# Moving the subtraction of the maximum from ScalarE to GpSimd in 48 of 128 attention units

## The reference, cut to what matters

```
# block 0                                       # block 1
scores = q @ k.T + mask                         scores = clip(q @ k.T * scale, -100, 100); masked: -inf
weights = softmax(scores, axis=-1)              attn = softmax(scores, axis=-1)
out = relu((weights @ v) @ wo.T + wo_b)         out = (attn @ v) @ wo.T + bo
```

## Time and profile before

| | us |
|---|---|
| median of 3 runs | 2119.77 |
| lowest, highest | 2115.42, 2124.47 |
| the profiled execution | 2117.64 |
| its span, first to last instruction | 2115.9 |
| busy in the span: PE, DVE, ACT, POOL | 1859.6, 1486.2, 1302.6, 616.5 |

### The profile page before, as it was taken

One profiled execution on the slowest core, in us unless ns is written; L12 is line 12 of the kernel. 1 busy time (PEld: TensorE's weight loads), 2 busy tenths in 40 slices (PEclk: granted clock), 3 DMA queues, 4 the chain that ended last, 5 costly groups with the idle time before them and its releaser, 6 DMA issues.

```text
span 2115.9 us, 49981 instructions
## 1 busy us (share of the span) xinstructions
PE 1859.6 (88%) x17665; PEld 1511.9 (71%) x17669; DVE 1486.2 (70%) x3873; ACT 1302.6 (62%) x4466; POOL 616.5 (29%) x610
## 2 busy tenths in 40 slices
PE   3998999989999897577898889999999998898879
PEld 2777888878888775455666677787777777677665
DVE  5898887878888785757666675767757565654556
ACT  1987766656667786456577766667666654544432
POOL 0003031322322220034333343254452523233321
PEclk9999999999999999868699999999999999999999
DMA  8013455444644001300000011222222223232351
GB/s 245 17 31 105 126 163 156 134 136 140 181 133 127 26 26 50 110 20 20 30 7 15 7 46 50 83 75 89 79 74 69 76 87 91 71 103 70 110 155 43
DMA packets 128789, 178.44 MB, mean 84 GB/s; under 512 B 10144, under 2 KB 89824, under 8 KB 128288
## 3 DMA queue, kind: packets, MB, share of 16 engines
q1 hardware_dynamic: 120864, 159.51, 25.0%
q0 software_dynamic: 7680, 15.74, 2.4%
HBM read 141.26 MB, written 33.95 MB: 83 GB/s over the span
## 4 chain that ended last, share of the span: by engine, by line
PE 38%; DVE 9%; ACT 6%; issue 4%; POOL 1%; DMA 0%; DVEq 0%; ACTq 0%; SPq 0%
PE ps L1674 5%; PE ps L1959 5%; PE ps L1907 3%; PE ps L1712 3%; PE ps L1900 3%; ACT pb L2108 3%; PE ps L1696 3%; PE ps L1881 2%; PE ps L1703 2%; PE ps L1685 2%; PE ps L1722 1%; DVE nm L2487 1%; PE ps L1730 1%; PE ps L1929 1%; PE ps L1873 1%
## 5 line engine op out<-in xcount | busy, mean ns | idle before, releaser
L2108 ACT ACTIVATE pb<-ps,nm 128x128 f32<-128x128 f32 x1024 | 363.1, 377 | 192.6 <-DVE nm L2487 192.5
L2156 POOL TENSOR_TENSOR pb<-pb,rcs 128x512 f32<-128x512 f32 x256 | 268.3, 1049 | 667.1 <-DVE rcs L2495 666.2
L986 ACT ACTIVATE pb<-pb,nm 128x128 f32<-128x128 f32 x1024 | 312.9, 393 | 30.9 <-DVE nm L1221 29.1
L2512 DVE COPY pt<-ps 128x512 f32<-128x512 f32 x128 | 88.3, 690 | 203.6 <-PE ps L1959 203.4
L2108 ACT ACTIVATION_READ_ACCUMULATOR pb<-ps,nm 128x1 f32 x1024 | 221.3, 216 | 0.0
L2487 DVE TENSOR_REDUCE nm<-ps 128x8 f32<-128x1024 f32 x128 | 155.9, 1218 | 62.2 <-PE ps L1907 39.0
L1959 PE MATMUL ps<-w,pb 128*128 128x128 f32 x1024 | 168.7, 290 | 21.9 <-ACT pt L2116 10.8
L1221 DVE TENSOR_REDUCE nm<-pb 128x8 f32<-128x1024 f32 x128 | 156.2, 1220 | 4.4
L1959 PEld LDWEIGHTS ps<-w,pb 128*128 128x128 f32 x1024 | 122.4, 148 | 46.3 <-ACT pt L2116 20.3
L870 PE MATMUL ps<-w,pb 128*128 128x128 f32 x1024 | 141.8, 280 | 8.2 <-ACT pb L986 7.9
L2116 ACT ACTIVATE pt<-ps 128x512 f32<-128x512 f32 x128 | 76.9, 601 | 94.9 <-PE ps L1959 94.6
(11 more groups left out here) (379 smaller groups left out, 4405.0 us busy)
## 6 DMA issues: line engine op xcount, KB each, us to landing
big<-in_we SPq DMA_DIRECT2D x92, 514.0 KB
big<-in_we SPq DMA_DIRECT2D x109, 384.0 KB
sorted_out<-big SPq DMA_DIRECT2D x27, 256.0 KB
big<-sorted_in SPq DMA_DIRECT2D x7, 960.0 KB, 5.7
sorted_in<-big SPq DMA_DIRECT2D x4, 1472.0 KB, 12.1
big<-sorted_in SPq DMA_DIRECT2D x20, 256.0 KB, 3.8
hidden<-h_all SPq DMA_DIRECT2D x7, 512.0 KB, 3.0
h_all<-hidden SPq DMA_DIRECT2D x7, 512.0 KB, 3.7
```

The costliest lines, as they stand in the source:

```text
L986: m = a.activation(pb[:, n % 2, k * S:(k + 1) * S], pb[:, n % 2, k * S:(k + 1) * S], ACT.Exp, bias=nm[:, n % 2, k:k + 1])
L2108: m = a.activation(pb[:, n % 2, e * S:(e + 1) * S], ps[:, score_bank(n) + half, k * S:(k + 1) * S], ACT.Exp, bias=nm[:, n % 2, e:e + 1], a ...
L2156: g_.tensor_tensor(p4, p4, r4.unsqueeze(2).to_broadcast([P, 4, S]), ALU.mult).then_inc(n2["p_normed"], 1)
L2512: v.tensor_copy(pt[:, p % 2, 4 * S:8 * S], ps[:, BANK_T, :]).then_inc(n2["p_lo"], 1)
```

## The change

In the units 1 to 26 and 106 to 127 (`SHIFTED`) the eight exponentials on ACT go. In their place POOL adds the negated maxima to the masked scores, in place in `pb`, in two instructions of 128 x 512 (four heads each). PE turns these shifted scores instead of the exponentials, and ACT forms the exponential while it empties the PSUM banks into `pt`, with the instructions that were copies before. The other 80 units (`BIASED`) stay as they were. Waits on the exponentials become waits on either semaphore (`formed`). To make room in POOL's order, the power for the front layernorm moves from unit 1 of a stream to unit 0 (from the third group on), ahead of the subtraction; and the eight gathers of the last group, which were four in unit 7 of stream 13 and four in unit 0 of stream 14 (steps 111 and 112), become two in each of the steps 110 to 113, behind the subtraction of their step.

```diff
+        GATHERS = [{-1: range(G), 0: range(G, 2 * G)}] * (NG - 1) + [{at: range(2 * at + 4, 2 * at + 6) for at in range(-2, 2)}]
+        SHIFTED = [n for n in range(NUN) if 1 <= n <= 26 or n >= 106]
+        BIASED = [n for n in range(NUN) if n not in SHIFTED]
...
+        def formed(n, half=1):
+            of = SHIFTED if n in SHIFTED else BIASED
+            return s["shifted" if n in SHIFTED else "exps"], 2 * of.index(n) + 1 + half
...
-                                pe.wait_ge(s["exps"], 2 * p + 1 + k // 4)
+                                pe.wait_ge(*formed(p, k // 4))
...
-                        a.activation(pt[:, p % 2, 0:4 * S], ps[:, 2, :], ACT.Copy).then_inc(s["p_hi"], 1)
+                        to_pt = ACT.Exp if p in SHIFTED else ACT.Copy
+                        a.activation(pt[:, p % 2, 0:4 * S], ps[:, 2, :], to_pt).then_inc(s["p_hi"], 1)
...
-                            a.activation(pt[:, p % 2, 4 * S:8 * S], ps[:, 3, :], ACT.Copy).then_inc(s["p_lo"], 1)
+                            a.activation(pt[:, p % 2, 4 * S:8 * S], ps[:, 3, :], to_pt).then_inc(s["p_lo"], 1)
                     work(1, n)
-                    if n < NUN:
+                    if n in BIASED:
                         a.wait_ge(s["maxed"], n + 1)
...
+                def shift(n):
+                    g_.wait_ge(s["maxed"], n + 1)
+                    for half in range(2):
+                        p4 = pb[:, n % 2, 4 * half * S:4 * (half + 1) * S].rearrange("p (k s) -> p k s", k=4)
+                        m4 = nm[:, n % 2, 4 * half:4 * half + 4]
+                        g_.tensor_tensor(p4, p4, m4.unsqueeze(2).to_broadcast([P, 4, S]), ALU.add)\
+                            .then_inc(s["shifted"], 1)
...
-                    if layer == 1 and u == 0:
-                        gather(g, range(G, 2 * G))
-                    if layer == 0 and u == 1:
+                    if layer == 0 and u == (0 if g > 1 else 1):
                         pow_(front, g + 1)
+                    if n in SHIFTED:
+                        shift(n)
+                    if layer == 1 and u in GATHERS[g]:
+                        gather(g, GATHERS[g][u])
...
-                    if layer == 1 and u == 7:
-                        g_.wait_ge(moe["stored"], 16 * NQ0 * (g // 2 + 1))
...
-                        gather(g, range(G))
+                    if layer == 1 and u - NU in GATHERS[g]:
+                        if min(GATHERS[g]) == u - NU:
+                            g_.wait_ge(moe["stored"], 16 * NQ0 * (g // 2 + 1))
...
+                        gather(g, GATHERS[g][u - NU])
...
-                            v.wait_ge(s["exps"], 2 * (n - 1))
+                            v.wait_ge(*formed(n - 2))
```

More of the change, by code:

```diff
@@ L297, in build @@
                       "p_lo", "pv", "o_recip", "normed", "oT_psum", "oT_ready", "out_psum", "bias_added"]
-        att_a = attention_sems("a", both_kinds + ["q_ready", "masked", "o_read", "o_turned"])
+        att_a = attention_sems("a", both_kinds + ["q_ready", "masked", "shifted", "o_read", "o_turned"])
         att_b = dict(att_a, **attention_sems("b", ["sums_turned", "p_normed", "k3_psum", "k3_col", "v_row", "chunk_added",
@@ L628, in build @@
                     last_evacuated = (moe["hid_dve" if k % 2 else "hid_act"], k // 2 + 1)
+        s = att_a
         spare_slots = h_all[:, 0:12, :].rearrange("p (a b) t -> p a b t", b=3)
@@ L1041, in _ @@
                     layer, g = stream(j + 2)
-                    if layer == 1 and u == 7:
-                        g_.wait_ge(moe["stored"], 16 * NQ0 * (g // 2 + 1))
-                        if g:
-                            g_.wait_ge(moe["gathered"], 16 * 2 * G * g)
-                            g_.wait_ge(moe["combined"], g)
-                        gather(g, range(G))
+                    if layer == 1 and u - NU in GATHERS[g]:
+                        if min(GATHERS[g]) == u - NU:
+                            g_.wait_ge(moe["stored"], 16 * NQ0 * (g // 2 + 1))
+                            if g:
+                                g_.wait_ge(moe["gathered"], 16 * 2 * G * g)
+                                g_.wait_ge(moe["combined"], g)
+                        gather(g, GATHERS[g][u - NU])
                 g_.wait_ge(moe["gathered"], 16 * 2 * G * NG)
```

## The result

Beside the kernel before on the same chip the changed kernel took 2136.5 us (median of 7 runs) against 2115.42: ratio 1.0105, interval 1.0086 to 1.0124. It is slower by 1.0%, as forecast (2140, range 2116 to 2160). The profiled execution took 2131.53 us, its span is 2129.8.

What follows compares the result with a forecast made beforehand. Plain units were taken to be at PE's floor of 3.77 us, loaded units bound by DVE. 25.6 - 7 + 11.2 - 6 - 2.2 = +21.6 us on 2117.64 gave 2139.2, rounded to 2140; range 2116 to 2160.

Steps and rivals of the forecast that it cites:

- the place of the loss: Loaded units: additions meet VectorE's SBUF-only work right behind the maximum; 25.6 and 11.2 us; PSUM work and statistics safe.
- the relief of ScalarE: Plain units, where VectorE does only division, mask and maximum: second half ready sooner, 0.13 us each, about 17 units, -2.2 us.
- moved pieces: Front power and last group's gathers on POOL: cost nothing; if POOL fell behind, 1 to 2 us once.
- additions: VectorE busy longer: VectorE held by additions in loaded units: 25.6 us in the first stretch, 11.2 in the second.
- the return: While VectorE is held PE catches up; 7 us of VectorE's idle time come back in the first stretch, 6 in the second.
- The block: One meeting in a loaded unit: 0.70 or 0.81 us for the first addition plus 1.04 for the second, 1.75.
- Which works are blocked: First stretch: 13 layernorms, queries, router steps and gates at 1.75 us, two residual sums together 2.8; 25.6 us.
- The second stretch: Units 106 to 127: five blocks 8.8 us, queries 1.4, expert outputs 0.5 each, together 11.2; 6 come back.
- rival C: PE idles in loaded units and its clock falls too, 0.92 us on scores each time; some 2155 us; chance 0.13.
- signs of being wrong: L345 and L1068 stay at 1.1 to 1.7 us, PE still waits before transposes, or first-stretch clock below 1.00.
- rival B: ACT was the bound: PE's waits for exponentials before its second four transposes, 10.0 us, go; 2108 us; chance 0.10.
- Rival A: Only one addition blocks, VectorE gets in before the second; block 0.75 us, about 2120, no change; chance 0.20.

Runs made afterwards that it cites:

- e8: Kernel before with only the moved power and gathers, no unit shifted; ratio 1.0002 to the kernel before.
- e3: Changed kernel with no addition on GpSimd, so the maximum is not subtracted in the 48 units; ratio 0.9937 to the kernel before.
- e4: Changed kernel with exponentials back on ScalarE and GpSimd's 96 additions made on constants into unread tiles; ratio 1.0114 to the kernel before.
- e7: Changed kernel with the last group's eight gathers put back where they were; ratio 1.0113 to the kernel before.
- e1: Changed kernel with only the 18 units shifted that have no other SBUF work right behind the maximum; ratio 0.9977 to the kernel before.
- e6: Kernel before with VectorE's other work a step later, between mask and maximum of the next unit; ratio 1.0176 to the kernel before.
- e9: Changed kernel with additions in loaded units waiting until VectorE begins the next step's division; ratio 1.0164 to the kernel before.

## Why the prediction was right, term by term

The sum was +21.6; the touched stretches show +22.1. The total is that near by luck: every term but the place of the loss was off, and the errors cancel. The experiments split it: e8 less before is the moves, e3 less e8 the relief of ScalarE, changed less e3 the additions. The last part is split once more, into VectorE's busy time and its idle time in the windows, since the prediction counted blocked time first and then took off what comes back.

| term | predicted | first | second | together |
|---|---|---|---|---|
| moved pieces | 0 | -0.1 | -4.4 | -4.5 |
| relief of ScalarE | -2.2 | -4.1 | -1.8 | -5.9 |
| additions: VectorE busy longer | +25.6 and +11.2 | +17.6 | +11.7 | +29.2 |
| additions: VectorE idle, the return | -7 and -6 | +0.4 | +2.9 | +3.3 |
| sum | +21.6 | +13.7 | +8.4 | +22.1 |

The windows of e3 that this rests on; those of the changed kernel stand in the section on the result:

```profile
49.26:155.67 106.41, 103.56 (x1265) 86.52 (x1264) 95.80 (x205) 39.77 (x85) 7.36 (x9) 1.00 0.08 24
708.28:804.62 96.34, 89.44 (x1068) 73.04 (x1069) 80.82 (x170) 34.82 (x72) 16.42 (x16) 0.98 0.06 17
```

The term of the additions holds all that they meet, the moved gathers among it. Of the -4.5 of the moves only the 1.95 of unit 114 are shown to be theirs (e8).

**The place of the loss: right.** SBUF work right behind the maximum meets the additions, in both stretches, and PSUM work doesn't: the mask L586 lasts at most 1226 ns and the statistics L329 at most 295 in the changed kernel. e4 shows the meeting by itself.

**The block: size a little high, its make-up wrong.** I took 0.70 for the first addition and 1.04 for the second "which follows at once", 1.75. Measured: 1.46 for layernorms, 1.56 for query masks (unit 4, 3.23 us in place of 1.67), 1.51 in the router (unit 16, 7.16 in place of 5.64); in the first case two instructions stretched by 0.73 each. The row of 2.18 us had misled me: there an indirect DMA stood first. Where that is so in the changed kernel, in unit 112, VectorE does wait through all three: one of the four instructions there takes 2.81 us, by the view by source line.

```profile
L345 DVE TENSOR_SCALAR y<-x_all,mv_last_ln,rs_last_ln x4: 334/336/2814, 761.8 to 765.1; 128x128 f32<-128x128 f32 x4
```

The Trainium skill ("SBUF — State Buffer", section "Who interferes with whom") says that, where VectorE is in a two-port mode, whoever issues first holds the shared ports for the whole instruction and the other is blocked in full. The trace agrees for one instruction, which lasts until just behind the end of the addition. What the prediction made of it for two in a row, 2.08 us, is too much in most units, since VectorE gets a turn between them.

**Which works are blocked: mostly right, but 8.0 us too many in the first stretch.** The residual sums cost next to nothing in place of 1.4 each (units 13 and 21: 5.95 and 5.95 us after, 5.92 and 5.83 before), and the gates of unit 18 as little in place of 1.75 (4.06 against 4.01). The query masks of unit 20 cost nothing in place of 1.75: there a copy on VectorE stands ahead of them, the four masks pass at the 1.65 us that they took before, and it is GpSimd's addition that waits.

```profile
139.94 0.67 DVE L1194 COPY big<-ps 8x512 f32<-8x512 f32 x1
140.10 2.99 POOL L1027 TENSOR_TENSOR pb<-pb,nm 128x512 f32<-128x512 f32 x1 [1.33 <-DVE nm L1241]
140.53 1.65 DVE L1088 TENSOR_SCALAR h_all<-qT,w 128x512 f32<-128x512 f32 x4
```

Instead L336, "safe" in the prediction, stretched in units 7, 15 and 23, which became 0.74, 0.39 and 0.40 longer. It reads and writes SBUF alone, as the layernorms do, and I had put it with L329 without a row of its own.

**The return: the step that failed.** The prediction let 7 and 6 us of VectorE's idle time come back, as PE catches up while VectorE is held. In single units this is there: unit 5 to 6 lasts 2.76 us (before 3.48), 8 to 9 lasts 2.76 (3.64), 10 to 11 lasts 3.17 (3.75), together 2.2 us. But it needs a plain unit behind the loaded one, and from unit 12 on every unit of the first stretch but unit 19 is loaded. Against the kernel before, VectorE's idle time fell by 3.1 us in the first stretch and by 2.8 in the second (102.50 less 81.31, then 110.90 less 92.47); against e3 it grew. So nothing came back that ScalarE's relief and the moves had not already given. The blocks, 29.2 us in place of 36.8, make up for it in the sum.

**The second stretch: blocks right in sum, return wrong.** VectorE's busy time rose by 11.2 us, as forecast, with unit 112 and its gather in it ("nothing" in the prediction). The idle time that grew against e3 lies in units 109 and 117, where PE ran at the lower clock. In units 108 and 116 the blocked layernorm is the input of a turn on PE. In the changed kernel PE waits 2.31 us for it in its step 117 and then runs its transposes in 1.85 us; in e7, where PE comes to it later, it waits 1.32 and they take 1.04. From 790.0 to 793.1 us the granted clock of the changed kernel was 0.50, the level of 1.2 GHz. The timelines of PE there, the changed kernel first, then e7:

```profile
788.54 0.66 PE L743 MATMUL ps<-w,y 128*128 128x128 f32 x4 [2.31 <-DVE y L345]
789.03 0.83 PE L876 MATMUL ps<-w 128*128 128x128 f32 x6
789.70 1.85 PE L878 MATMUL ps<-w,pb 128*128 128x128 f32 x8
```

```profile
790.75 0.66 PE L743 MATMUL ps<-w,y 128*128 128x128 f32 x4 [1.32 <-DVE y L345]
791.25 0.83 PE L876 MATMUL ps<-w 128*128 128x128 f32 x6
791.92 1.04 PE L878 MATMUL ps<-w,pb 128*128 128x128 f32 x8
```

Unit 117 to 118 lasts 5.55 us in the first, 4.04 in the second, 4.03 before; unit 109 to 110, behind the same wait of 2.31 us, 5.69 in place of 4.15. That is rival C, not in place of the blocks but on top of them, where PE has idled: the granted clock is 0.95 and 0.94 in the two stretches of the changed kernel, and 1.00 and 0.98 in e3. A clock below 1.00 in the first stretch was one of the prediction's signs of being wrong, and it showed; but there it cost next to nothing. The whole fall lies in two pairs of units, 16 and 17, 24 and 25, and in their windows VectorE is busy for all but 0.34 and 0.35 us:

```profile
118.97:131.37 12.40, 12.17 (x121) 9.82 (x121) 12.06 (x21) 3.43 (x9) 4.28 (x4) 0.72 0.01 1
160.78:173.79 13.01, 13.01 (x119) 11.08 (x119) 12.66 (x23) 3.56 (x9) 4.29 (x4) 0.74 0.00 1
```

So of the 32.5 us that the additions cost, 29.2 are VectorE's longer busy time, and about 3 are the two units of the second stretch behind PE's fallen clock.

**ACT's relief: too small, and in another place.** I gave it to plain units alone, 2.2 us. e1 less e8 shows none there (-0.4 and +0.5). e3 less e8 gives 5.9, with no addition to wait for; changed less e4, with the additions in both, gives 4.4 (127.89 less 124.33, 111.74 less 110.90), half of it in unit 20 (8.11 and 5.90). So rival B's mechanism is there, with 4 to 6 of its 10.0 us, and the additions outweigh it five to one or more. **Rival A**, that only one addition blocks, is refuted by the 1.46 of unit 9 and by the source line view: two instructions wait. The plain units of the end (122 to 125) last 3.75 to 3.85 us, as said.

No kernel here beats the kernel before by 0.5%, but e3, which leaves out a part of the reference's computation. Of the others, e1 is lowest (0.9977); in its profiled execution the gain lies in the second stretch, which is as short in e8, and in units 26 to 106, where its code is that of e8 (546.35 us there, 552.35 in e8), so I don't put it down to the shifted units.

## What to carry to other kernels

Moving work from a busy engine to an idle one is priced by what the idle engine's instructions meet, not by its idle time: list what VectorE does, in SBUF alone, in the stretch in which GpSimd will run, and multiply the instructions that wait by what is left of a GpSimd instruction when they start. Time lost so comes back only where a unit with slack follows. Moving either side out of the other's way has a price too: ahead of the maximum it delayed the chain by more (e6), behind the work it delayed PE by more (e9). A total that comes out right proves no term: kernels that each do one part (moves only, relief only, additions only) and VectorE's busy and idle time apart showed here that the blocks had been put 7.6 us too high, and that 13 us were to come back of which none did.

## What the runs showed of the hardware

- In most meetings on SBUF one VectorE instruction passed for each GpSimd addition, and a waiting VectorE instruction was stretched by one addition less some 0.3 us (0.73 with additions of 1.04, 0.30 with 0.59, 1.61 with 1.90).
- In others none passed: an instruction waited through two additions in e7's unit 113 (1.98 us in place of 0.42) and through an indirect DMA and two additions in unit 112 of the changed kernel (2.81 us in place of 0.34). What makes the difference is open.
- GpSimd's side of a meeting varied as widely: an addition of 1.04 us took 1.07 and 1.03 beside the layernorm of e4's unit 9, and 2.99 in unit 20, where VectorE's copy and four query masks passed first.
- An instruction of 128 x 4 was blocked like a large one: L336 took 0.91 us in place of 0.17.
- ScalarE's exponential of 128 x 512 on the way out of PSUM costs what the copy did, 597 ns on average against 596; an addition took 1087 ns on average over all 96, the waits above included. The page, costliest groups:

```profile
L1027 POOL TENSOR_TENSOR pb<-pb,nm 128x512 f32<-128x512 f32 x96 | 102.4, 1087 | 111.3 <-DVE nm L1241 111.3
...
L987 ACT ACTIVATE pt<-ps 128x512 f32<-128x512 f32 x128 | 76.5, 597 | 91.7 <-PE ps L878 91.0
```
